# Latent attention with mean squares in four 128x32 tiles and roots spread by transfers; expert row fetches all ahead of sends

## The reference, cut to what matters

```python
# latent attention (third attention); B=4 batches, S=512 tokens, 77 context keys, 16 heads of 64
xn = layernorm(layernorm(x));  cn = layernorm(context)
q = rmsnorm(xn @ Wq) * qn_g          # per head, over its 64 numbers
k = rmsnorm(concat(cn, xn) @ Wk) * kn_g
v = concat(cn, xn) @ Wv
out = softmax(q @ k.T * 64**-0.5) @ v
x = x + gate * (out @ Wout + bout)
# rmsnorm(t) = t / max(sqrt(mean(t*t)), eps) * gamma
# 64 experts, top 3, at most 64 tokens each
y[token, k] = gelu(x[token] @ w1[e] + b1[e]) @ w2[e] + b2[e]
x = x + gate * sum_k(g[token, k] * y[token, k])
```

## Time and profile before

| what | value |
|---|---|
| median of 3 runs | 1460.13 us (1458.07 to 1470.2) |
| time of the profiled execution | 1467.86 us |
| its span, one core | 1465.3 us, of which 2.6 us lie outside |
| granted TensorE clock, mean | 0.957 of full speed |
| busy over the span: TensorE, VectorE, ScalarE, GpSimd | 89%, 56%, 48%, 35% |

### The profile page before, as it was taken

How to read it: one execution, slowest core, us unless ns; L and a number is a source line. 1 busy time by engine, 2 the same in 40 slices (tenths; PEclk the granted TensorE clock), 3 DMA queues, 4 the chain that set the end, 5 groups by cost and what they waited for, 6 DMA issues and landing times. The chain is left out here.

```text
span 1465.3 us, 19896 instructions
## 1 busy us (share of the span) xinstructions
PE 1311.1 (89%) x7055; PEld 567.5 (39%) x7055; DVE 827.5 (56%) x1364; ACT 700.0 (48%) x1216; POOL 514.9 (35%) x486
## 2 busy tenths in 40 slices
PE   5888789659996899999999999999976998887998
PEld 2213332238972333333333333333334774323443
DVE  3757767272337666656665666566445444623654
ACT  4454444442225666656665666566432444453222
POOL 1012201046621744444554454445414771320000
PEclk9999899779999999999999999999997999898999
DMA  9500310159622000000000000000042124000430
GB/s 260 220 1 12 101 21 1 65 184 383 247 85 87 1 1 1 1 0 2 0 1 0 1 1 1 1 1 1 1 154 62 52 53 130 1 1 1 116 74 15
DMA packets 40109, 85.75 MB, mean 59 GB/s; under 512 B 7582, under 2 KB 23070, under 8 KB 39262
## 3 DMA queue, kind: packets, MB, share of 16 engines
q1 hardware_dynamic: 28044, 70.44, 14.6%
q0 software_dynamic: 4544, 9.32, 2.3%
q10 hardware_dynamic: 7424, 4.72, 1.1%
HBM read 76.56 MB, written 11.04 MB: 60 GB/s over the span
## 5 line engine op out<-in xcount | busy, mean ns | idle before, releaser
L2652 ACT ACTIVATE a_prob<-a_TP 128x512 f32<-128x512 f32 x256 | 138.9, 594 | 123.4 <-PE a_TP L2423 121.7
L2787 DVE TENSOR_REDUCE a_lat<-a_SP 128x2 f32<-128x1024 f32 x128 | 155.7, 1216 | 62.6 <-PE a_SP L2387 62.5
L2915 POOL TENSOR_TENSOR a_acc<-a_prob 128x512 f32<-128x512 f32 x64 | 79.8, 1269 | 232.5 <-ACT a_prob L2652 232.5
L2419 PE MATMUL a_TP<-a_qn,a_kn 64*128 64x512 f32 x512 | 147.5, 641 | 2.6 <-ACT a_prob L2652 2.6
L2435 PE MATMUL a_MS<-a_prob,a_V 128*64 128x512 f32 x512 | 122.6, 599 | 0.2 <-ACT a_prob L2652 0.2
L3470 DVE TENSOR_REDUCE a_nm<-a_A 128x8 bf16<-128x616 f32 x84 | 66.7, 794 | 38.3 <-PE a_A L3153 38.2
L2924 POOL TENSOR_TENSOR a_acc<-a_acc,a_prob 128x512 f32<-128x512 f32 x64 | 80.0, 1274 | 18.4 <-ACT a_prob L2652 18.4
L2419 PEld LDWEIGHTS a_TP<-a_qn,a_kn 64*128 64x128 f32 x512 | 40.4, 184 | 104.3 <-issue 75.3
L2919 POOL TENSOR_TENSOR a_acc<-a_acc,a_prob 77x512 f32<-77x512 f32 x64 | 80.4, 1277 | 0.0
L3684 POOL TENSOR_TENSOR a_on<-a_osb,a_rden 128x512 f32<-128x512 f32 x9 | 11.5, 1280 | 162.6 <-ACT a_osb L3353 162.6
L2423 PE MATMUL a_TP<-a_negm,onesb 64*128 64x512 bf16 (+1 forms) x320 | 64.8, 377 | 0.0
(11 more groups left out here) (553 smaller groups left out, 2856.3 us busy)
## 6 DMA issues: line engine op xcount, KB each, us to landing
ring_w<-in_F_w SPq DMA_DIRECT2D x64, 512.0 KB, 9.1
f_wide<-weight_rows SPq DMA_DIRECT2D x24, 256.0 KB, 5.5
a_maskT<-in_maskT SPq DMA_DIRECT2D x1, 2304.0 KB
a_biasT<-in_biasT SPq DMA_DIRECT2D x1, 2304.0 KB
f_b<-in_F_b SPq DMA_DIRECT2D x1, 2048.0 KB, 9.4
token_rows<-f_xtok ACTq DMA_DIRECT2D x8, 256.0 KB, 8.1
a_biasQ<-in_biasQ SPq DMA_DIRECT2D x3, 616.0 KB, 5.3
ring_w<-expert_rows SPq DMA_DIRECT2D x4, 384.0 KB, 6.2
```

Source lines behind the costliest of these rows:

```text
L2419: nc.tensor.matmul(TP[0:n, h, :], keys(h), qn[half(h), r % 4, :], start=True, stop=False)
L2652: nc.scalar.activation(prob[0:n, 2 * k + h, :], TP[0:n, h, :], ACT.Exp, bias=rowneg[0:n, b:b + 1] if k == 0 else 0.0).then_inc(p_ready, 1)
L2787: nc.vector.tensor_reduce(lat[:, g % 2, 2 * u:2 * u + 2], SP[:, :, :], AX.X, ALU.max, negate=True).then_inc(s_used, 1)
L2915: nc.gpsimd.tensor_tensor(acc[:, h, :], prob[:, 2 + h, :], prob[:, 4 + h, :], ALU.add).then_inc(added, 1)
```

## The change

In the latent attention, from round 3's tensors on (`RAW` = 3):
- `means` uses four tiles of 128 rows by 32 columns, one for each of q and k and each half (256) of the tokens. The weights are 32 columns of `blk`: 16 that add up head 0 and 16 for head 1. The result has 128 partitions x 256 columns in one bank of MS (the first), with 16 equal rows for each head, tensor and half. `square_k` becomes one instruction instead of two, `clip_means`, Ln and Exp work on 128x256 instead of 128x1024.
- The roots (`rms_rows`) are spread to the 64 partitions of each head, in `rn`, by eight transfers from SBUF to SBUF on SyncE's queue: four for q, then four for k (64 partitions x 1 KB each). `norm_q` and `norm_k` wait for four of them each.
- The order of the round: the projection goes to step 0, `values(r - 1, 3)` and the means to step 1, `values(r - 1, 4)` and `sums(r - 1)` to step 2, `later_values` to step 4. `values(r, 0)` to `values(r, 2)` stay in step 3. In rounds 8, 16 and 24 the output goes to step 3 and these values to step 4. ScalarE and VectorE follow: the denominators' logarithm behind the exponentials of step 2, `normalise` behind the last 128-token maxima, `norm_k` directly behind `norm_q`, and `shift` behind the reduction of `maxima(r + 2, 0)`.

With 64 experts, each pair has its own row buffer (32 of them, used for the fetched rows and then for the results), GpSimd issues all fetches first and then all sends.

```diff
-                    for n in range(AHEAD, PAIRS + AHEAD):
-                        if n < PAIRS:
-                            if n >= FETCH:
-                                pool.wait_ge(rows_turned, n - FETCH + 1)
-                            fetch(n)
-                        if n - AHEAD >= 2:
-                            send(n - AHEAD - 2)
...
+                    for n in range(ROUTED, PAIRS):
+                        fetch(n)
                     pool.wait_ge(c.rows_zeroed, 32)
+                    for n in range(PAIRS):
+                        send(n)
...
+                for g in range(RAW, R):
+                    sp.wait_ge(ms_rms, g + 1)
+                    for j, normed, spread in ((0, q_normed, q_spread), (1, k_normed, k_spread)):
+                        sp.wait_ge(normed, g)
+                        for n in range(2):
+                            for h in range(2):
+                                at = 32 * (2 * j + n) + 16 * h
+                                sp.dma_start(rn[half(h), j, n * HS:(n + 1) * HS],
+                                             rms_rows[at:at + 16, :].rearrange("i (c t) -> i c t", c=1)
+                                             .broadcast_to([16, 4, HS])).then_inc(spread, 16)
...
+                    if g >= RAW:
+                        for j in range(2):
+                            for n in range(2):
+                                at = 32 * (2 * j + n)
+                                mm = nc.tensor.matmul(MS[at:at + 32, 0, 0:HS], blk[:, HD - 16:HD + 16],
+                                                      mine[:, j, n * HS:(n + 1) * HS], start=True, stop=True)
+                        mm.then_inc(ms_ready, 1)
+                        return
...
+                        if s == 2 and r:
+                            values(r - 1, 4)
+                            if r + 3 < R:
+                                pe.wait_ge(ms_clipped, r + 4)
+                            sums(r - 1)
...
+                        nc.scalar.activation(rms_rows[:, :], lnn[:, 0, 0:HS], ACT.Exp, scale=-0.5)\
+                            .then_inc(ms_rms, 1)
...
                 def norm_q(g):
-                    dve.wait_ge(ms_rms, g + 1)
+                    if g >= RAW:
+                        dve.wait_ge(q_spread, 64 * (g - RAW + 1))
+                    else:
+                        dve.wait_ge(ms_rms, g + 1)
```

More of the change, by code:

```diff
@@ L1602, in capacity_moe @@
             src, dest = sb("src", [P, PAIRS], U32), sb("dest", [P, PAIRS], U32)
-            xs = sb("xs", [P, FETCH, D])
+            rows = [sb(f"row{n}", [P, D]) for n in range(ROUTED)]
             b_loaded, lists_ready = sem("b_loaded"), sem("lists_ready")
-            rows_in = [sem(f"rows_in{i}") for i in range(FETCH)]
+            rows_in = [sem(f"rows_in{n}") for n in range(PAIRS)]
             def fetch(n):
                 nc.gpsimd.indirect_dma_start(
-                    out=xs[:, n % FETCH, :], out_offset=None, in_=c.xrows[:, :],
-                    in_offset=bass.IndirectOffsetOnAxis(ap=src[:, n:n + 1], axis=0)).then_inc(rows_in[n % FETCH], 16)
+                    out=rows[n][:, :], out_offset=None, in_=c.xrows[:, :],
+                    in_offset=bass.IndirectOffsetOnAxis(ap=src[:, n:n + 1], axis=0)).then_inc(rows_in[n], 16)
             with ExitStack() as own:
@@ L1931, in capacity_moe @@
             hb, hg = sb("hb", [P, 2, 512]), sb("hg", [P, 2, 512])
-            ys = sb("ys", [P, SEND, D])
+            rows += [sb(f"row{n}", [P, D]) for n in range(ROUTED, PAIRS)]
             HP = ctx.enter_context(nc.psum_tensor(name + "_HP", [P, 2, 512], F32))
@@ L2140, in latent_attention @@
     R = B * NP
+    RAW, HS = 3, S // 2
     with ExitStack() as ctx, c.phase():
@@ L2514, in _ @@
                             maxima(r + 2, 0)
-                        if s == 0 and r:
-                            values(r - 1, 3)
-                            values(r - 1, 4)
-                            sums(r - 1)
-                            if r < 2 * B:
-                                later_values(r)
                         if s == 0 and r == 0:
                             variance(4)
-                        if s == 1 and r + 3 < R:
+                        if s == (0 if r else 1) and r + 3 < R:
                             if has_values(r - 1):
@@ L2528, in _ @@
                             project(r + 3)
-                        if s == 2:
+                        if s == 1 and r:
+                            values(r - 1, 3)
+                        if s == (1 if r else 2):
                             if r == 0:
@@ L2554, in _ @@
                                 make_values(r)
+                            if 0 < r < 2 * B:
+                                later_values(r)
+                            if p == 0 and b:
+                                pe.wait_ge(x_updated, b)
+                                for k in range(3):
+                                    values(r, k)
                 values(R - 1, 3)
```

127 lines of the change are left out of this document (66 added, 61 removed).

## The result

The changed kernel takes 1470.74 us, median of 20 runs (1467.23 to 1478.93), the kernel before 1465.76 us on the same chip, median of 20 runs (1458.07 to 1514.26). The ratio is 1.005, with a 95% interval from 1.0035 to 1.0066: about 0.5% slower, and well within the 1% that I called no change; two slow runs of the kernel before, 1507.05 and 1514.26 us, are left out of it. Two more measurements gave 1.0055 (1.0031 to 1.0079) and 1.005 (1.0027 to 1.0074). The profiled execution took 1475.93 us with a span of 1474.1; that of before 1467.86 and 1465.3.

The account below looks back on a forecast made before the run. TensorE's work and waits bound the kernel. Ordinary rounds +4.6, output rounds -3.8, round 0 +3.1, last rounds +0.5 and experts 0 sum to +4.4 us on the 1460.13 median: 1464.5 us, range 1447 to 1482.

Parts of the forecast that it names:

- the start: Round 0 of the latent attention: late clip, roots and k transfers delay `negm`, +3.1 us once, +5.5 with late landing.
- the ordinary rounds: 24 latent attention rounds (1 to 27 without 8, 16, 24): 17.29 us each against 17.10, together +4.6 us.
- the outputs: Rounds 8, 16, 24: the clip wait goes, one for `normalise` comes, 24.4 us against 25.67, together -3.8 us.
- the last rounds: Last four rounds: round 28 loses the values block covering `shift`, round 30 gains a little, +0.5 us.
- wait for `normalise`: Step 3 of every round: `values(r, 0)` waits 0.65 us, with only 2.51 us of matmuls covering the chain behind the sums.
- Rival 1: No wait for `normalise`: rounds of 16.64 us, sum -13.7 us, kernel 1446.4 us; chance 12%.
- The split: Values divided between steps 1 and 2: 0.08 x 28 = 2 us by the rows, 0 if tile-shape changes are free.
- `norm_q` and `norm_k` do not wait after round 0: VectorE: after round 0 the spread's q and k transfers land before their two consumers need them.
- the 2.8 us of room: Spread: k lands 13.0 us into the round and may land as late as 15.8 before anyone waits.
- Rival 2: Spread lands late, k at 17.0 us into the round, 1.2 too late in 28 rounds: +34 us, about 1500 us; 14%.
- rival 3: The means' four new 128-row tiles do not run side by side: +1.3 us in step 1, +36 us, 1500 us; 4%.
- Experts: 64 experts: TensorE stays fully busy with all fetches ahead of sends, 0 us, bounds -1 and +2.

Follow-up runs that it names:

- `sums_first`: Changed kernel with `sums(r - 1)` ahead of `values(r - 1, 4)` in step 2: 1453.53 us against 1462.77 for the kernel before, ratio 0.9928.
- `shift_first`: Changed kernel with round 0's reduction of `maxima(2, 0)` and `shift(1)` ahead of `norm_q` and `norm_k`: 1466.31 us in one profiled run.
- `keys_later`: Changed kernel with four more transfers into a spare tile between q's and k's, `norm_k` waiting for them too: 1596.02 us, one run.
- `moe_alone`: Kernel before with only the experts' change (a row buffer per pair, all fetches before all sends): 1464.95 us against 1462.77, ratio 1.0011.
- `best`: Changed kernel with sums ahead of `values(r - 1, 4)` and the spread from round 4's tensors: 1537.25 us against 1511.55 for the kernel before, ratio 1.0177.
- `best_again`: Changed kernel with sums ahead of `values(r - 1, 4)` and `RAW` = 4, in a later measurement: 1449.73 us against 1465.54 before, ratio 0.9904.
- `old_order`: Changed kernel's new means and spread, but in the kernel before's order of the round: 1629.04 us against 1511.55 before, ratio 1.0789.

## Why the prediction was right

The forecast was 1464.5 us, no change, against a median of 1460.13; that median rests on three runs, and over 20 runs the same kernel lies at 1465.76. In differences the forecast was +4.4 us and the medians say +5.0. The two traces differ by 8.8, of which 1.4 is the fall of the clock at the start; the profiled run of the changed kernel lay 5.2 above its own median.

That +4.4 meets the +5.0 of the medians so well is in part luck. My terms are those of the rounds, and these grew by 8.9, 7.6 and 8.1 us in the three pairs of traces, about twice my sum. Term by term, for the first pair: the start +6.4 for my +3.1, the ordinary rounds +6.0 for +4.6, the outputs -3.6 for -3.8, the last rounds 0 for +0.5. The medians of the three measurements differ by 5.0, 6.0 and 5.7; what takes the other 2 to 3 us out of the whole times the runs don't show. "No change within 1%" would have been right with either sum.

- **The wait for `normalise`** is there in 28 rounds and in front of the three outputs, 0.60 us from start to start where I had 0.65: from the sums' start the chain takes 3.11 us (I had 3.16), and TensorE's cover is the 2.51 of the prediction (0.96 to the scores, 1.55 to the values). `sums_first` shows that it decides. Rival 1, no such wait at 16.64 per round, did not come; where `sums_first` takes the wait away the round is 16.80, not 16.64.
- **The ordinary round** was put at 17.29 and is 17.41, though the wait is a little shorter: its work is 16.80 to my 16.64. The lone values cost 1.01 (761.38 to 762.39) and 0.91, where I had 0.91 and 0.88, the means 0.57 for 0.53. The term "24 rounds x 0.19" was thus mis-sized: 17 x 0.30 and 6 x 0.16. (Round 1 stands in the start here.) Rounds 2 to 7 lose less, 0.16: the change also puts their two blocks, of values and of the context's values, directly behind each other, where they take 0.92 and 0.95, and in before each stood alone between scores and took 1.01 and 1.02. I had set both down at the same price. Together that makes 6.0 for my 4.6.
- **The Trainium skill**, "TensorEngine Tiling (Array Packing)", Key Properties, says that a change of the tile mode drains TensorE. The trace agrees: four passes of values take 0.88 within a run of the same tiles, 0.91 with a change of tiles only in front (the values of step 2, followed by the sums), and 1.01 with a change in front and behind (those of step 1, between maxima and means). The split cost about 0.16 us per round (1.01 + 0.91 against 1.76). My text gave 0.08 as its price, from the earlier trace rows, and my sum held only 0.03 of it, since I took 0.91 for the lone value and 0.88 for the other.
- **Rounds 8, 16, 24**: forecast -1.3 each, measured -1.19, for the reason given.
- **The start** was the step that was most off: +3.1 forecast, +5.0 without and +6.4 with the fall of the clock, which my sum had no term for. Two terms were too small, an issue of 0.62 us (5.00 over 8) where I took 0.46 and a landing of 2.4 where I took 2.0; both lay within the bounds of the rows. Seven steps of 0.16 and 0.4 put the last of k 1.5 us later. And I followed only the chain through `negm`; the block of later values waits for `norm_q`, 2.1 us, ahead of it, which `shift_first` leaves standing.
- **"`norm_q` and `norm_k` do not wait after round 0"** was wrong for `norm_k`: it waits in all 29 rounds, for 0.29 us in the round shown. It lies in VectorE's free time, so the sum was not touched; but of the 2.8 us of room only 1.1 were left.
- **Rival 2** (late spread) and **rival 3** (tiles not side by side) did not come: the eight matmuls of the means cost 0.57 together, and `keys_later` shows that rival 2's chain decides once k lands over 1.1 us later still.
- **The last rounds**: +0.5 forecast, 0 measured. **Experts**: 0 forecast, +0.2 in the trace, and nothing in `moe_alone` that stands out of its interval.

## What to carry to other kernels

When work between a reduction and its consumer is made shorter or moved away, count what is left as cover for the chain that runs on the other engines beside it: here 2.51 us of matmuls against 3.1 of chain, and 0.6 us in each of 31 rounds ate the whole gain of cheaper means. Put the instruction that starts such a chain ahead of independent work in an in-order queue; two groups exchanged turned a kernel 0.5% slower than before into one 0.7% faster than before. A spread by small transfers is paid in issue time and landing, 0.6 us each and 2.4 us here, so eight of them want some 7 us between the roots and their use (an estimate: 8 x 0.62 + 2.4), and a first round that has no such room should keep the old way.

## What the runs showed of the hardware that was not expected

Eight transfers from SBUF to SBUF that each write 64 KB, in pieces of 1 KB, need 5.0 us of one queue, 0.54 us at the least for one, and each takes 2.3 to 3.7 us to land. Four more of them crossed the edge of a loop of 17.4 us.

The same two waits of TensorE, 2.1 us and, some 2 us of work later, 1.1 to 1.9, are followed by the lower clock (0.57 and 0.58) in two traces of the changed kernel and by the full clock in a third and in `sums_first`. In `keys_later` a wait of 1.97 us was followed by 0.61 and one of 1.94 us, a round later, by 1.00. What decides was not found.

In one measurement the kernel before took 1511.55 us, not 1465, and the three traces taken there, all of kernels with the new order of the fetches, show two stages stretched. The first is the one with 64 experts: from its first matmul to the attention's first it takes 201.8 us in `best` (279.07 to 480.91), against 166.7 in `best_again` (282.00 to 448.66). Single matmuls stand there with up to 2.4 us of issue between them (time in which TensorE waits for nothing that the profile shows), from 333 to 364 us:

```profile
356.04 0.37 PE L2014 MATMUL f_YP<-ring_w,f_hg 128*64 128x128 f32 x1 [2.43 <-issue]
```

Between 345 and 375 us the granted clock was 0.50 and the busy time 14.5 of 30 us in `best`, against 30 of 30 in `best_again`:

```profile
345.00:375.00 30.00, 14.54 (x71) 11.74 (x72) 2.86 (x6) 2.05 (x5) 13.35 (x14) 0.50 0.43 138
```

```profile
345.00:375.00 30.00, 30.00 (x326) 27.08 (x325) 9.83 (x20) 7.83 (x20) 22.68 (x25) 1.00 1.02 385
```

The second is the feed forward part behind the latent attention, which the change doesn't touch: 193.5 us in `best` (1096.80 to 1290.33), against 149.0 in `best_again` (1066.01 to 1214.98). In `best` groups stand behind issue time here too:

```profile
1148.21 1.62 PE L1041 MATMUL f_YP<-f_W,f_hvT 128*128 x6 [3.88 <-issue]
```

On the same chip, later, the changed kernel took 1471.14 and the kernel before 1465.43, so the condition came and went, and is not the chip's own. It isn't a matter of the new kernel alone either, since the kernel before was slow in that measurement too, and in two of its 20 runs in the first (1507.05 and 1514.26).

Does the new order of the fetches make it worse? No trace of the kernel before was taken there, so it isn't shown, but the numbers speak for it. The kernel before lost 46 us (1511.55 against 1465), about what the second stage alone lost in `best`, 44.5. The three others lost more than their attention explains. By the traces, `best` is 15 to 18 us shorter in the attention than the kernel before, and its median was 26 longer; `keys_later` is 53 to 56 longer there and took 84 more; `old_order` 82 to 86, and took 117 more. That leaves 28 to 44 us in each, and the stage with 64 experts lost 35 in each (201.8, 201.6 and 201.8 us). So the experts' half of the change, neutral in every other measurement, probably costs some 35 us in this condition. What would settle it is a trace of the kernel before, or of `moe_alone`, taken in that condition.
